# Second attention of a two-layer model: the values of four units in one run, the context normalised late, odd narrow units turned into the other bank

## The reference

```python
q, k, v = (proj(q_w), proj(k_w), proj(v_w))            # 16 heads of 8 channels
scores = jnp.einsum('bhid,bhjd->bhij', q, k) / scale
alibi = -distance[None, :, :] * _slopes(N_HEADS)[:, None, None]
scores = jnp.where(causal[None, None], scores + alibi[None], -jnp.inf)
attn = jax.nn.softmax(scores, axis=-1)
out = jnp.einsum('bhij,bhjd->bhid', attn, v)
return out.transpose(0, 2, 1, 3).reshape(b, l, D_MODEL) @ o_w
```

## Time and profile before

| | |
|---|---|
| median of 3 runs | 2506.7 us (2501.7 to 2507.82) |
| profiled execution | 2507.11 us |
| its span | 2505.4 us |
| mean granted clock of TensorE over the span | 0.982 |
| busy over the span: TensorE, VectorE, ScalarE, GpSimd | 90%, 76%, 69%, 34% |
| the second attention | from about 1965 us to the end |
| the same shares from 2013.6 to 2272.9 us | TensorE 241.23, VectorE 231.55, ScalarE 241.37 of 259.30 us |

### The profile page before, as it was taken

How to read it: one execution, slowest core, us unless ns; L and a number is a source line. 1 busy time by engine, 2 the same in 40 slices (tenths; PEclk the granted TensorE clock), 3 DMA queues, 4 the chain that set the end, 5 groups by cost and what they waited for, 6 DMA issues and landing times. The chain is left out here.

```text
span 2505.4 us, 90533 instructions
## 1 busy us (share of the span) xinstructions
PE 2250.0 (90%) x34464; PEld 1764.0 (70%) x34464; DVE 1914.7 (76%) x7571; ACT 1736.3 (69%) x5614; POOL 843.7 (34%) x911
## 2 busy tenths in 40 slices
PE   6999998799988899899899888779999699999998
PEld 5888887577777777777777676558777466666665
DVE  6777772567777778777777777658888588898888
ACT  2333332677777777777777777866666599999998
POOL 3666665020122211211112212221212556566562
PEclk9999999899999999999999999989999799999999
DMA  7857452666667666676667664013231111111110
GB/s 245 236 157 196 110 117 45 161 163 166 171 165 177 169 173 170 164 171 166 162 173 173 172 168 122 17 66 113 94 117 69 47 27 42 30 36 38 27 38 14
DMA packets 360772, 304.77 MB, mean 122 GB/s; under 512 B 25368, under 2 KB 328856, under 8 KB 358952
## 3 DMA queue, kind: packets, MB, share of 16 engines
q1 hardware_dynamic: 349864, 271.93, 42.6%
q0 software_dynamic: 10496, 27.28, 3.7%
HBM read 166.43 MB, written 132.69 MB: 119 GB/s over the span
## 5 line engine op out<-in xcount | busy, mean ns | idle before, releaser
L823 ACT ACTIVATE probs<-neg_scores,low 128x256 f32<-128x256 f32 (+1 forms) x1152 | 574.3, 500 | 244.2 <-DVE low L959 226.2
L959 DVE CUSTOM_DVE_ANT_0 neg_scores<-scores,rel_bias 128x256 f32<-128x256 f32 x1024 | 373.7, 421 | 244.3 <-PE scores L1121 126.7
L1135 PE MATMUL probsT<-consts,probs 128*128 128x128 f32 x2240 | 361.5, 284 | 54.2 <-ACT probsT_s L839 49.3
L1135 PEld LDWEIGHTS probsT<-consts,probs 128*128 128x128 f32 x2240 | 248.7, 142 | 111.8 <-ACT probsT_s L839 72.4
L774 POOL TENSOR_SCALAR q_heads<-q_raw,consts,q_bias 128x256 f32<-128x256 f32 x128 | 69.7, 558 | 746.6 <-ACT q_raw L805 746.5
L1685 DVE CUSTOM_DVE_ANT_0 neg_scores<-scores,alibi 128x128 f32<-128x128 f32 (+1 forms) x896 | 265.9, 352 | 57.4 <-PE scores L1741 53.5
L275 POOL TENSOR_TENSOR hid<-hid,gate_bc 128x512 f32<-128x512 f32 x160 | 205.7, 1291 | 151.9 <-DVE hid L448 141.9
L301 ACT ACTIVATE ga<-gate_up 128x512 f32<-128x512 f32 x160 | 95.6, 598 | 223.7 <-PE gate_up L514 208.5
L967 DVE COPY rel_s<-scores 128x768 f32<-128x768 f32 x256 | 244.0, 953 | 5.2 <-PE scores L1121 3.8
L1647 ACT ACTIVATE probs<-neg_scores,low 128x128 f32<-128x128 f32 (+1 forms) x448 | 199.6, 448 | 47.7 <-DVE low L1685 45.7
L1111 PE MATMUL scores<-k_sides,q_heads 32*128 32x256 f32 (+1 forms) x2304 | 205.5, 424 | 26.9 <-DVE rel_s L967 21.0
(11 more groups left out here) (205 smaller groups left out, 4942.6 us busy)
## 6 DMA issues: line engine op xcount, KB each, us to landing
rel_rows<-rel_s SPq DMA_DIRECT2D x256, 192.0 KB
rel_bias<-rel_rows SPq DMA_DIRECT2D x256, 192.0 KB, 3.4
gate_bc<-gate_rows SPq DMA_DIRECT2D x32, 1024.0 KB, 10.1
rel_rows<-rel_s SPq DMA_DIRECT2D x256, 128.0 KB
rel_bias<-rel_rows SPq DMA_DIRECT2D x256, 128.0 KB, 3.0
packed<-ffn_in SPq DMA_DIRECT2D x8, 1280.0 KB, 15.0
xe<-packed SPq DMA_DIRECT2D x16, 640.0 KB, 3.9
expert_out<-ye POOLq DMA_DIRECT2D x16, 640.0 KB, 3.2
```

The lines of the kernel that those rows point to most:

```text
L823: act.activation(probs[s % 3][:, j, 0:w], neg[s % 2][:, j, 0:w], ACT.Exp, bias=low[s % 3][:, j:j + 1], scale=-1.0, accum_out=sums[s // UB ...
L959: dve.tensor_tensor_reduce(neg[s % 2][:, j, 0:w], S_ps[:, 512 * j:512 * j + w], bias_of(s)[:, j, :] if s < NU0 else alibi[:, 4 * j + s % 4 ...
L1135: ins = pe.transpose(PT_ps[:, j * P:(j + 1) * P], probs[u % 3][:, j, kt * P:(kt + 1) * P], ident)
```

## The change

The change keeps every instruction's kind, and moves where three of the engines do some of them.

- TensorE no longer does `value(u)` in each step. `values(g)` does all four units of a group in one run, 16 matmuls for a narrow group and 32 for a wide one, then the turned inverse sums, at the end of steps 6 (narrow group) and 2 (wide group of the batch before). `valued` now counts groups.
- In TensorE's step the projections stand ahead of `score(s + 1)`, no longer behind it.
- `probsT` holds the four units of a group, in two buffers, instead of three buffers of a unit.
- Narrow units with an odd number are turned into `PT_ps[1]`, and ScalarE copies them; even ones stay with VectorE. `moved` is one counter for each bank.
- VectorE normalises the context after its copy and the inverse sums of the step, no longer at the start of the step.

```diff
@@ -1462,7 +1462,7 @@
             neg = [sbb(f"neg_scores1_{i}", [P, 4, S]) for i in range(3)]
             low = [sbb(f"low1_{i}", [P, 4]) for i in range(3)]
             probs = [sbb(f"probs1_{i}", [P, 4, S]) for i in range(3)]
-            probsT = [sbb(f"probsT1_s{i}", [P, KT, 4, P]) for i in range(3)]
+            probsT = [sbb(f"probsT1_s{i}", [P, 4, KT, 4, P]) for i in range(2)]
             sums = [sbb(f"sums1_{i}", [P, 4, 4]) for i in range(2)]
             rinv = sbb("rinv1", [P, H])
             rinv_c = sbb("rinv1_c", [P, H, C])
@@ -1485,8 +1485,7 @@
             lowest = semb("lowest_ready")
             exped = semb("probs_ready")
             turned = semb("probsT_ready")
-            moved0 = semb("probsT_first_half_moved")
-            moved1 = semb("probsT_second_half_moved")
+            moved = [semb(f"probsT_bank{k}_moved") for k in range(KT)]
             valued = semb("values_ready")
             one_inverse = semb("inverse_sums_of_heads")
             inverted = semb("inverse_sums_ready")
@@ -1516,6 +1515,15 @@
 
             def wide_before(u):
                 return u // UB * 4 + max(0, u % UB - 4)
+
+            def bank_of(u, kt):
+                return kt if half_of(u) else u % 2
+
+            def moved_before(u, k):
+                return sum(1 for v in range(u) for kt in range(half_of(v) + 1) if bank_of(v, kt) == k)
+
+            def turned_with(u, kt):
+                return u + wide_before(u) + kt + 1
 
             job_list = [(-2, "qk", 0), (-1, "v", 0)]
             for b in range(NB + 1):
@@ -1627,7 +1635,7 @@
                         if b < 2:
                             act.wait_ge(zeros_set, 2)
                         else:
-                            act.wait_ge(valued, UB * (b - 1))
+                            act.wait_ge(valued, 2 * (b - 1))
                         for a in range(KT):
                             to = v_of[b % 2][:, a, :, :]
                             ins = act.copy(bass.AP(tensor=to.tensor, offset=to.offset, ap=[to.ap[0], [D + C, 4], [32, 4], [1, C]]),
@@ -1648,11 +1656,12 @@
                                            bias=low[s % 3][:, j:j + 1], scale=-1.0,
                                            accum_out=sums[g % 2][:, j, i:i + 1]).then_inc(exped, 1)
                     u = s - 2
-                    if 0 <= u < NU1 and half_of(u) == 1:
-                        act.wait_ge(turned, u + 1 + wide_before(u + 1))
-                        if u >= 3:
-                            act.wait_ge(valued, u - 2)
-                        act.copy(probsT[u % 3][:, 1, :, :].rearrange("p g q -> p (g q)"), PT_ps[1][:, :]).then_inc(moved1, 1)
+                    if 0 <= u < NU1 and (half_of(u) or u % 2):
+                        kt = half_of(u)
+                        act.wait_ge(turned, turned_with(u, kt))
+                        if u >= UB:
+                            act.wait_ge(valued, u // 4 - 1)
+                        act.copy(probsT[u // 4 % 2][:, u % 4, kt, :, :].rearrange("p g q -> p (g q)"), PT_ps[1][:, :]).then_inc(moved[1], 1)
                     if 0 <= s < NU1:
                         for j in range(2, 4):
                             act.wait_ge(lowest, 4 * s + j + 1)
@@ -1665,15 +1674,6 @@
             @block.vector
             def _(dve):
                 for s in STEPS:
-                    if s >= 7 and s % 4 == 3 and s // 4 - 1 < 2 * NB:
-                        g = s // 4 - 1
-                        dve.wait_ge(valued, 4 * (g + 1))
-                        dve.tensor_copy(rinvT[:, :], O_ps[:, P:2 * P]).then_inc(inverse_moved, 1)
-                        dve.wait_ge(inverse_moved, g + 1)
-                        if g >= 4:
-                            dve.wait_ge(spare_full, job_no["out", g // 2 - 2])
-                        dve.tensor_tensor(ctxT[g // 2 % 2][:, g % 2 * P:(g % 2 + 1) * P], O_ps[:, 0:P], rinvT[:, :],
-                                          ALU.mult).then_inc(normed, 1)
                     if 0 <= s < NU1:
                         w, i = width(s), s % 4
                         dve.wait_ge(scored, s + 1)
@@ -1686,19 +1686,29 @@
                                                      alibi[:, 4 * j + i, S - w:S], 1.0, 3e38, ALU.add, ALU.min,
                                                      low[s % 3][:, j:j + 1]).then_inc(lowest, 1)
                     u = s - 2
+                    if 0 <= u < NU1 and (half_of(u) or u % 2 == 0):
+                        dve.wait_ge(turned, turned_with(u, 0))
+                        if u >= UB:
+                            dve.wait_ge(valued, u // 4 - 1)
+                        dve.tensor_copy(probsT[u // 4 % 2][:, u % 4, 0, :, :].rearrange("p g q -> p (g q)"), PT_ps[0][:, :]).then_inc(moved[0], 1)
                     if 0 <= u < NU1:
-                        dve.wait_ge(turned, u + 1 + wide_before(u))
-                        if u >= 3:
-                            dve.wait_ge(valued, u - 2)
-                        dve.tensor_copy(probsT[u % 3][:, 0, :, :].rearrange("p g q -> p (g q)"), PT_ps[0][:, :]).then_inc(moved0, 1)
                         if u % 4 == 3:
                             g = u // 4
                             dve.wait_ge(exped, 16 * (g + 1))
                             dve.reciprocal(rinv[:, :], sums[g % 2][:, :, :].rearrange("p j i -> p (j i)")).then_inc(one_inverse, 1)
                             dve.wait_ge(one_inverse, g + 1)
                             if g >= 1:
-                                dve.wait_ge(valued, 4 * g)
+                                dve.wait_ge(valued, g)
                             dve.tensor_copy(rinv_c[:, :, :], rinv[:, :].unsqueeze(2).to_broadcast((P, H, C))).then_inc(inverted, 1)
+                    if s >= 7 and s % 4 == 3 and s // 4 - 1 < 2 * NB:
+                        g = s // 4 - 1
+                        dve.wait_ge(valued, g + 1)
+                        dve.tensor_copy(rinvT[:, :], O_ps[:, P:2 * P]).then_inc(inverse_moved, 1)
+                        dve.wait_ge(inverse_moved, g + 1)
+                        if g >= 4:
+                            dve.wait_ge(spare_full, job_no["out", g // 2 - 2])
+                        dve.tensor_tensor(ctxT[g // 2 % 2][:, g % 2 * P:(g % 2 + 1) * P], O_ps[:, 0:P], rinvT[:, :],
+                                          ALU.mult).then_inc(normed, 1)
                     for name, b in jobs_at.get(s - 1, ()):
                         if name == "out":
                             dve.wait_ge(spare_full, job_no[name, b])
@@ -1745,43 +1755,40 @@
                 def turn(u):
                     pe.wait_ge(exped, 4 * (u + 1))
                     for kt in range(half_of(u) + 1):
-                        if kt == 0 and u >= 1:
-                            pe.wait_ge(moved0, u)
-                        if kt == 1 and wide_before(u):
-                            pe.wait_ge(moved1, wide_before(u))
+                        k = bank_of(u, kt)
+                        if moved_before(u, k):
+                            pe.wait_ge(moved[k], moved_before(u, k))
                         for j in range(4):
-                            ins = pe.transpose(PT_ps[kt][:, j * P:(j + 1) * P], probs[u % 3][:, j, kt * P:(kt + 1) * P], ident)
+                            ins = pe.transpose(PT_ps[k][:, j * P:(j + 1) * P], probs[u % 3][:, j, kt * P:(kt + 1) * P], ident)
                         ins.then_inc(turned, 1)
 
-                def value(u):
-                    b, g, i = u // UB, u // 4, u % 4
-                    pe.wait_ge(moved0, u + 1)
-                    if half_of(u):
-                        pe.wait_ge(moved1, wide_before(u + 1))
-                    if i == 0 and g >= 1:
+                def values(g):
+                    b, n = g // 2, g % 2 + 1
+                    for k in range(KT):
+                        pe.wait_ge(moved[k], moved_before(4 * g + 4, k))
+                    if g >= 1:
                         pe.wait_ge(normed, g)
-                    if u % UB == 0:
+                    if g % 2 == 0:
                         pe.wait_ge(spare_free, job_no["v", b])
-                    n = half_of(u) + 1
-                    for kt in range(n):
-                        for j in range(4):
-                            rows = slice(32 * j, 32 * j + 32)
-                            ins = pe.matmul(O_ps[rows, 0:P], v_of[b % 2][:, kt, i, rows], probsT[u % 3][:, kt, j, :],
-                                            start=(i == 0 and kt == 0), stop=(i == 3 and kt == n - 1), skip_group_check=True)
-                    if i == 3:
-                        pe.wait_ge(inverted, g + 1)
-                        ins = pe.transpose(O_ps[:, P:2 * P], rinv_c[:, :, :].rearrange("p h c -> p (h c)"), ident)
-                    ins.then_inc(valued, 1)
+                    for i in range(4):
+                        for kt in range(n):
+                            for j in range(4):
+                                rows = slice(32 * j, 32 * j + 32)
```

(13 more changed lines are left out.)

## The result

The changed kernel takes 2521.94 us (median of 7 runs, 2515.67 to 2528.53), the kernel before 2506.6 (7 runs): ratio 1.0066, 95% interval 1.0051 to 1.0081. It is slower, as forecast, by 15 us where 24 were forecast. Its profiled execution took 2522.25 us, its span is 2520.6.

What follows compares the result with a forecast made beforehand. Each interval between score starts was the larger of score loop and TensorE's list, plus VectorE lateness: 19.39 against 18.51 us per batch, 26 x 0.88 = 22.9, plus 1 at the end, on 2507.1 gives 2531 us; range 2510 to 2548.

Steps and rivals of the forecast that it cites:

- score loop: From a unit's score start through VectorE's four minima to the next score start: 1.55 us narrow, 2.30 wide.
- interval 3 to 4: Between score starts of units 3 and 4: score, wide run, inverse, turn and value projection on TensorE, 3.77 us.
- The pause of 0.17 after an idle score: On TensorE, a narrow score costs 0.60 instead of 0.43 us when TensorE idled before it.
- Interval 7 to 0: From score 7 to the next batch's score 0: score, narrow run, inverse and wide turn on TensorE, 2.89 us.
- 0 to 1: Between score starts of units 0 and 1: loop 1.55 plus VectorE 0.16 late, 1.71 us.
- 1 to 2: Between score starts of units 1 and 2: score, wide turn, query and key projection on TensorE, 2.57 us.
- A group in a run: Four value matmuls inside TensorE's run of values: 0.21 us each, bounds 0.19 to 0.36.
- (b): Rival: a group in TensorE's run costs 0.12 us, so no difference can be told, 2507 us; chance 0.06.
- (d): Rival: a group in TensorE's run pays its weight loads in line, 0.40 us, giving 2590 us; chance 0.02.
- Odd narrow units: Two copies per batch from VectorE to ScalarE: VectorE's relief worth nothing, ScalarE's 0.92 us covered by TensorE's stall.
- Rival (a): The busiest engine sets the pace, not the score waits; floor is ScalarE's 18.15 us a batch, 2497 us; chance 0.10.
- Rival (c): ScalarE on the path: its 0.92 us adds to every batch, giving 2555 us; chance 0.06.

Runs made afterwards that it cites:

- e6: Changed kernel with the projections again behind score(s + 1), on a chip where the kernel before takes 2511.7 us; ratio to the kernel before 1.0015.
- e4: Kernel before with only its projections moved ahead of score(s + 1); ratio to the kernel before 1.0020.
- e2: Changed kernel with every unit's first half turned into bank 0 and copied by VectorE, as before the change; ratio to the kernel before 1.0079.
- e7: Changed kernel with projections behind the scores and all first halves copied by VectorE; ratio to the kernel before 1.0104.
- e1: Changed kernel with the projections again behind score(s + 1), on a chip where the kernel before takes 2705 us; ratio to the kernel before 1.0104.
- e9: Changed kernel with projections behind the scores and one reciprocal that spreads the inverse sums itself, without the copy; ratio to the kernel before 1.0102.

## Why the prediction was right

**What bounds.** Right. Every interval of every kernel is the score loop (1.55, 2.30), TensorE's list, or VectorE late; those of the changed kernel from score 4 to 7 are 2.30, as forecast.

**Sum of the batch.** 19.39 forecast, 19.14 measured, so +0.88 for +0.63. The 15 us are accounted for: batches 2 to 26 give 25 x 0.59 = 14.8 in the mean, batch 1 is 1.2 shorter, and from the last score to the end it takes 1.3 longer (forecast: 1). The mis-sized term is interval 3 to 4, 3.77 for 3.46. The pause of 0.17 after an idle score isn't paid when the run follows (2133.44 to 2133.88 is 0.44), and behind the long run the inverse took 0.17 for 0.26 and the turn 0.43 for 0.53. The run itself was 0.05 longer than worked out. Interval 7 to 0 was 0.10 under for the same reason, 0 to 1 and 1 to 2 were 0.07 over each: VectorE was 0.23 late for 0.16, and the wide turn of step 1 also waited for ScalarE's exponentials (0.19 at 2129.93). Pieces priced behind short neighbours are priced too high behind a long one.

**A group in a run**, 0.21: measured 0.22; rivals (b) at 0.12 and (d) at 0.40 fall with it, and with (d) the rule on weight loads that the prediction quotes from the Trainium skill, for these shapes.

**Which part costs.** Here the text was off, though its intervals held. It said that where the runs stand counts more, and booked the projections as a mere move. e6 shows that the move costs 0.94 in a regular batch (0.46 in the mean), and the run with late normalising and ScalarE's copies gains 0.31 without it. In the old order (e4) the same move costs 0.54, so how the 0.63 is shared out depends on which part is taken first. The run looked guilty since interval 3 to 4 holds both. The prediction's own prices held the answer: with the projections behind the scores they give 1.71 + 1.60 + 1.93 + 3.22 + 6.90 + 2.89 = 18.25, under the 18.51 of before. That sum wasn't made.

**Odd narrow units**, taken as worth nothing: 0.1 (e2) in this order. Right here, and wrong for the order of e6, where the turn behind the run makes VectorE's step 3 late (0.55, e7).

**Rival (a)**, the busiest engine: the kernel with ScalarE 18.09 of 19.14 busy is the slower one, so it fell. In e6's regular batch, 18.20, ScalarE is 17.99 busy, and there it would be next. **Rival (c)** fell with e2.

## What to carry to other kernels

Where a matmul waits for the buffer that the last one filled, list what stands between the two on the in-order engine, and compare each interval with the loop: work is free only in intervals that have room, and a small piece moved by one place can cost more than a large one saves (here 0.94 against 0.31). When a sum of several moves comes out as a loss, make it again without each of them. Price a moved part in the order it will have, not in the one it leaves. Before an engine is relieved, ask what will be idle then: here shorter lists went with falls of TensorE's clock, and brought a VectorE copy beside GpSimd's product more often.

## What the runs showed of the hardware

A VectorE copy of 128x128 took 0.23 us alone and 0.98 beside a GpSimd product (tensor_tensor) of 1.05, and a reciprocal of that size 0.94 where 128x16 took 0.24. TensorE's clock fell to 1.2 GHz for 3 to 4 us within a batch of e6 in which it was busy 17.66 of 19.41 us, and no pause of it shortly before was over 1.0 us. And the same program takes 2507 and 2512 us on two chips and 2705 on two others, with pauses of VectorE of up to 4.4 us (e1, e9) that no instruction of it accounts for.
